# The folded matrix M in three split passes, and two feed-forward weights loaded and split later

## The reference, cut to what matters

```python
attn = jnp.einsum('bhik,bhjk->bhij', q, k)      # self-attention, 8 heads, no softmax
out = jnp.einsum('bhik,bhkj->bhij', attn, v)
...
scores = jnp.where(Mask == 0, jnp.float32(NEG_INF), scores)   # cross-attention
attn = jax.nn.softmax(scores, axis=-1)
...
r = jax.nn.sigmoid(jnp.einsum('btc,dc->btd', xr, W_r))        # feed-forward
k_act = jnp.square(jax.nn.relu(jnp.einsum('btc,dc->btd', xk, W_k)))
out = r * jnp.einsum('btc,dc->btd', k_act, W_v)
```

## Time and profile before

| what | before |
|---|---|
| median of 3 runs (lowest to highest) | 927.52 us (927.21 to 927.59) |
| time of the profiled execution | 927.58 us |
| its span | 925.8 us |
| TensorE matmuls busy | 908.7 us, 98% |
| weight loads, DVE, ACT, POOL busy | 730.2, 707.6, 545.4, 500.9 us |
| granted TensorE clock, mean | 0.998 |
| moved by DMA | 45.65 MB, 49 GB/s on average |

### The profile page before, as it was taken

One profiled execution on the slowest core, in us unless ns is written; L12 is line 12 of the kernel. 1 busy time (PEld: TensorE's weight loads), 2 busy tenths in 40 slices (PEclk: granted clock), 3 DMA queues, 4 the chain that ended last, 5 costly groups with the idle time before them and its releaser, 6 DMA issues.

```text
span 925.8 us, 18979 instructions
## 1 busy us (share of the span) xinstructions
PE 908.7 (98%) x6694; PEld 730.2 (79%) x6694; DVE 707.6 (76%) x1985; ACT 545.4 (59%) x1658; POOL 500.9 (54%) x505
## 2 busy tenths in 40 slices
PE   8999998999999999999999999999999999999997
PEld 7867566667787878888888787878787878787876
DVE  6697456457797979787887878787878787879775
ACT  6555206657665757575856666656575757575631
POOL 1034015657675666657575756666566665756420
PEclk9999999999999999999999999999999999999999
DMA  8791000103000000002101010101010010100001
GB/s 293 244 336 48 23 26 29 38 8 108 15 24 31 25 31 24 31 24 81 29 25 30 25 30 25 30 25 30 24 29 25 12 43 8 47 1 24 1 23 46
DMA packets 30890, 45.65 MB, mean 49 GB/s; under 512 B 2764, under 2 KB 15564, under 8 KB 30540
## 3 DMA queue, kind: packets, MB, share of 16 engines
q1 hardware_dynamic: 26139, 35.26, 11.9%
q10 hardware_dynamic: 4656, 9.18, 2.9%
HBM read 34.10 MB, written 9.70 MB: 47 GB/s over the span
## 4 chain that ended last, share of the span: by engine, by line
PE 73%; DVE 6%; issue 4%; POOL 3%; ACT 2%; POOLq 0%; DVEq 0%; ACTq 0%
PE dense L88 18%; PE dense L90 17%; PE dense L89 17%; PE turned L1501 5%; PE scores L1489 4%; PE rest_value L1515 3%; PE rest_value L1519 3%; PE turned L1398 1%; PE dense L1398 1%; PE rest_value L1507 1%; PE scores L1404 1%; DVE prob L1041 1%; POOL row_inv L1304 1%; ACT prob L756 1%; PE dense L1443 1%
## 5 line engine op out<-in xcount | busy, mean ns | idle before, releaser
L1304 POOL TENSOR_TENSOR row_inv<-row_sum,minus_one 128x4 f32<-128x4 f32 x128 | 145.6, 1138 | 262.5 <-ACT prob L756 260.9
L756 ACT ACTIVATE prob<-prob,row_min 128x154 f32<-128x154 f32 x512 | 209.4, 417 | 20.4 <-DVE row_min L1041 20.4
L1310 POOL TENSOR_TENSOR prob<-prob,row_inv 128x512 f32<-128x512 f32 x128 | 136.4, 1065 | 0.0
L1041 DVE CUSTOM_DVE_ANT_0 prob<-scores,mask_add 128x154 f32<-128x154 f32 x512 | 127.0, 309 | 6.3 <-PE scores L1489 6.2
L764 ACT ACTIVATE prob_t<-turned 128x512 f32<-128x512 f32 x128 | 75.8, 592 | 53.1 <-PE turned L1501 53.1
L756 ACT ACTIVATION_READ_ACCUMULATOR prob<-prob,row_min 128x1 f32 x512 | 98.8, 193 | 0.0
L1501 PE MATMUL turned<-ident,prob 128*128 128x128 f32 x512 | 77.0, 273 | 3.7 <-POOL prob L1310 1.4
L88 PE MATMUL dense<-xt_hi,cross_wq_hi 128*128 128x256 f32 x256 | 75.2, 294 | 1.3 <-DVE xt_lo L1032 1.3
L88 PE MATMUL dense<-mix_k_hi,ffn_wk_hi 128*128 128x256 f32 x256 | 74.6, 291 | 0.0
L1501 PEld LDWEIGHTS turned<-ident,prob 128*128 128x128 f32 x512 | 61.0, 141 | 15.8 <-issue 4.7
L1099 DVE TENSOR_TENSOR k_act_lo<-square,k_act_hi 128x512 fp32r<-128x512 f32 x32 | 51.4, 1606 | 28.8 <-ACT k_act_hi L789 28.8
(11 more groups left out here) (273 smaller groups left out, 2658.9 us busy)
## 6 DMA issues: line engine op xcount, KB each, us to landing
x_rows<-x_rows SPq DMA_DIRECT2D x32, 256.0 KB, 4.4
xt_raw<-x_cols SPq DMA_DIRECT2D x16, 512.0 KB, 3.7
out<-gate_then_y SPq DMA_DIRECT2D x15, 512.0 KB, 2.8
mask_in<-mask SPq DMA_DIRECT2D x16, 154.0 KB, 2.3
cross_wv<-cross_wv SPq DMA_DIRECT2D x2, 512.0 KB, 6.8
cross_wk<-cross_wk SPq DMA_DIRECT2D x1, 1024.0 KB, 9.3
self_wv<-self_wv ACTq DMA_DIRECT2D x1, 1024.0 KB, 8.0
self_wk<-self_wk ACTq DMA_DIRECT2D x1, 1024.0 KB, 11.8
```

The source lines that it names most:

```text
L756: m = act.activation(keys, keys, ACT.Exp, bias=row_min[:, buf, t, h:h + 1], scale=-1.0, accum_out=row_sum[:, buf, t, h:h + 1])
L1041: m = dve.tensor_tensor_reduce(prob[buf][:, t, h * CTX:(h + 1) * CTX], s_bank[:, h, t * CTX:(t + 1) * CTX], mask_add[n % 2][:, t, :], -SCA ...
L1304: pool.tensor_tensor(row_inv[:, buf, t, :], row_sum[:, buf, t, :], minus_one[:], ALU.pow).then_inc(*p_inv.up)
L1310: pool.tensor_tensor(keys[:, :, 0:P], keys[:, :, 0:P], inv.broadcast_to([P, HPG, P]), ALU.mult).then_inc(*p_norm.up)
```

## The change

M's quarters of both batches become three-pass products. For that self_wq is split in the prologue, and u0 and u1 are split in four parts each by ACT and DVE. The places for these parts are those of feed-forward weights, so ffn_wk and ffn_wr are no longer loaded and split in the prologue: ffn_wk is loaded first of all in the rounds and split in round -1; ffn_wr is loaded in round 1 once M is made, ahead of the write of M; ffn_wv follows, once ffn_wr has landed; both are split in round 2, at other places than ffn_wv was. The diff, cut to its core:

```diff
-    early = ("cross_wq",) + LATE_WEIGHTS[:-1]
+    early = ("cross_wq", "cross_wo")
+    splits = [weights[name] for name in early] + [(f["self_wq"], *wq_two)]
...
-            for name in early[2:]:
-                load_weight(name)
-            for i in range(len(early)):
+            for i in range(len(splits)):
                 weight_high(i)
                 high(2 * i + 24, 2 * i + 25)
+            high(30, 31)
             for q in range(KT):
                 act.wait_ge(*u_mm.at(0, q + 1))
                 act.activation(u0[:, q, :], u_bank[q][:], ACT.Copy).then_inc(*u_ok.up)
+            for q in range(KT):
+                act.wait_ge(*u_ok.at(0, q + 1))
+                act.activation(u0_two[0][:, q, :], u0[:, q, :], ACT.Copy).then_inc(*u_ok.up)
...
-            weight_low(3)
             low(30, 31)
...
+            c_times(0, 0)
+            c_times(1, 1)
+            for q in range(KT):
+                dve.wait_ge(*u_ok.at(0, KT + q + 1))
+                dve.tensor_tensor(u0_two[1][:, q, :], u0[:, q, :], f32(u0_two[0][:, q, :]), ALU.subtract).then_inc(
+                    *c_part_ok.up)
+            c_times(2, 2)
+            c_times(3, 3 + KT)
...
-                    m = pe.matmul(m_bank[i][:], f["self_wq"][:, q, i * P:(i + 1) * P], u0[:, q, :],
-                                  start=(q == 0), stop=(q == KT - 1))
+                    m = three_pass(pe, m_bank[i][:], [x[:, q, i * P:(i + 1) * P] for x in wq_two],
+                                   [x[:, q, :] for x in u0_two], first=(q == 0), last=(q == KT - 1))
...
             pe.wait_ge(*u_ok.at(0))
-            pe.wait_ge(*f_here["self_wq"].at(0))
+            pe.wait_ge(*c_part_ok.at(0, 2 + KT))
+            pe.wait_ge(*w_low.at(2))
...
+            load_weight("ffn_wk")
             load_mask(0)
...
                 if n == 1:
+
+                    sp.wait_ge(*fm_mm.at(0))
+                    load_weight("ffn_wr")
                     sp.wait_ge(*fm_eye.at(0))
                     sp.dma_start(m_park.rearrange("p (k n) -> p k n", k=KT), t1[:]).then_inc(*m_parked.up)
-                    sp.wait_ge(*fm_mm.at(0))
-                    sp.dma_start(raw["ffn_wv"][:], io["ffn_wv"].rearrange("(k p) n -> p k n", p=P)).then_inc(*w_here.up)
+                    load_weight("ffn_wv")
...
+            weight_high("ffn_wk")
             for n in range(-1, LAST):
...
                     if n == 2:
-                        weight_high()
+                        weight_high("ffn_wr")
...
                     r_gate(e, 0)
+                    if n == 2:
+                        weight_high("ffn_wv")
                     r_gate(e, 1)
...
+                if n == 0:
+                    u_high()
                 if live(n):
                     exponentials(n, 3, 0)
...
                     o_finish(f, 1)
+                if n == 2:
+                    weight_low("ffn_wr")
                 if live(f):
                     normalise(2, f, x2[f % 2])
...
                     masked_min(n, 2, 1)
-                    if n == 2:
-                        weight_low()
...
                     make_mask(a)
+                if n == 2:
+                    weight_low("ffn_wv")
                 x1t_low(a, 0)
...
                     take_t(3)
+                    weight_low("ffn_wk")
...
                     bias_u(2, 3)
+                    u_low()
...
                 if i == 0:
+                    pe.wait_ge(*fc_part.at(0))
                     pe.wait_ge(*q_out.at(1, 2))
...
-                    m = pe.matmul(m_bank[i], fold["self_wq"][:, c, i * P:(i + 1) * P], u1[:, c, :],
-                                  start=(c == 0), stop=(c == KT - 1))
+                    m = three_pass(pe, m_bank[i], [x[:, c, i * P:(i + 1) * P] for x in wq_two],
+                                   [x[:, c, :] for x in u1_two], first=(c == 0), last=(c == KT - 1))
...
-            "u": [mem.over("x1_0", "u0", square), mem.over("ffn_wv_hi", "u1", square)],
+            "u": [mem.over("x1_0", "u0", square), mem.over("ffn_wr_lo", "u1", square)],
+            "u_two": [(mem.over("ffn_wk_hi", "u0_hi", square, 0, F32R), mem.over("ffn_wk_lo", "u0_lo", square, 0, F32R)),
+                      (mem.over("ffn_wv_hi", "u1_hi", square, 0, F32R), mem.over("ffn_wr_lo", "u1_lo", square, 0, F32R))],
+            "wq_two": (mem.over("ffn_wr_hi", "self_wq_hi", square, 0, F32R), mem.over("ffn_wv_lo", "self_wq_lo", square, 0, F32R)),
```

More of the change, by code:

```diff
@@ L223, in weight_high @@
             def weight_high(i):
-                raw, hi, _ = weights[early[i]]
-                act.wait_ge(*w_here[early[i]].at(0))
+                raw, hi, _ = splits[i]
+                act.wait_ge(*(w_here[early[i]] if i < len(early) else f_here["self_wq"]).at(0))
                 act.activation(hi[:], raw[:], ACT.Copy).then_inc(*w_high.up)
@@ L307, in weight_low @@
             def weight_low(i):
-                raw, hi, lo = weights[early[i]]
+                raw, hi, lo = splits[i]
                 dve.wait_ge(*w_high.at(i))
@@ L375, in dve_program, with c_times @@
             low(28, 29)
-            weight_low(3)
             low(30, 31)
-            dve.wait_ge(*biases_in.at(0))
-            for q in range(KT):
+            def c_times(q, at):
                 dve.wait_ge(*u_ok.at(0, q + 1))
@@ L584, in layers @@
     g1, t1, kv_t1, u1 = (fold[x][1] for x in ("g", "t", "kv_t", "u"))
+    u1_two, wq_two = fold["u_two"][1], fold["wq_two"]
     s_col, s_part, c_part = (fold[x] for x in ("s_col", "s_part", "c_part"))
@@ L716, in act_program, with weight_high @@
         def act_program(act):
-            def weight_high():
-                act.wait_ge(*w_here.at(0))
-                act.activation(w["ffn_wv"][0][:], raw["ffn_wv"][:], ACT.Copy).then_inc(*w_hi_ok.up)
+            def weight_high(name):
+                act.wait_ge(*w_here.at(late.index(name)))
+                act.activation(w[name][0][:], raw[name][:], ACT.Copy).then_inc(*w_hi_ok.up)
             def take_u(*parts):
@@ L724, in take_u, with u_high @@
                     act.activation(u1[:, k, :], (d1, d0)[k % 2][:], ACT.Copy).then_inc(*fu_ok.up)
+            def u_high():
+                for k in range(KT):
+                    act.wait_ge(*fu_ok.at(0, k + 1))
+                    act.activation(u1_two[0][:, k, :], u1[:, k, :], ACT.Copy).then_inc(*fu_ok.up)
             def take_m(i):
@@ L977, in bias_u, with u_low @@
                                                  ALU.mult, ALU.add).then_inc(*fc_part.up)
+            def u_low():
+                dve.wait_ge(*fc_part.at(0, KT))
+                for k in range(KT):
+                    dve.wait_ge(*fu_ok.at(0, KT + k + 1))
+                    dve.tensor_tensor(u1_two[1][:, k, :], u1[:, k, :], f32(u1_two[0][:, k, :]), ALU.subtract).then_inc(
+                        *fc_part.up)
             def take_c():
@@ L1552, in k_product @@
             def k_product(n, h):
+                if n + h == 0:
+                    pe.wait_ge(*w_lo_ok.at(late.index("ffn_wk")))
                 pe.wait_ge(*mix_lo["k"].at(n))
@@ L1566, in r_product @@
             def r_product(n, t):
+                if n + t == 0:
+                    pe.wait_ge(*w_lo_ok.at(late.index("ffn_wr")))
                 if t == 0:
@@ L1582, in v_product @@
                 if n + t == 0:
-                    pe.wait_ge(*w_lo_ok.at(0))
+                    pe.wait_ge(*w_lo_ok.at(late.index("ffn_wv")))
                 pe.wait_ge(*ka_lo_ok.at(n))
```

30 lines of the change are left out of this document (18 added, 12 removed).

## The result

The changed kernel takes **932.08 us** (median of 7 runs, 929.62 to 935.54) against 927.59 for the kernel before on the same chip (927.21 to 928.33). The ratio is 1.0048, 95% interval 1.003 to 1.0065: half a per cent slower, where 926.2 had been forecast in a range of 924.2 to 928.9. So the time lies outside the range, on the slow side. Besides the 4.5 us there is a second thing to see: its runs lie 5.9 us apart, those of the kernel before 1.1.

What follows compares the result with a forecast made beforehand. TensorE, busy 98% of the span, was taken as the bound. The terms -0.7 + 1.4 + 0.2 - 2.1 - 0.25 = -1.45 took 927.58 to 926.2 us, range 924.2 to 928.9.

Steps and rivals of the forecast that it cites:

- The products, 2.73 us a quarter, and -0.70 each: M products on TensorE: three passes take 2.73 us a quarter instead of 3.43, saving 0.70 each.
- Quarters 0, 1 and 2 will end 2.1 us sooner, then TensorE stands still before the sums: Prologue, batch 0: the 2.1 us saved become waiting before batch 1's column sums; only quarter 3 counts, -0.70.
- The mask comes 2.8 us later: Start of the rounds: first mask queued behind ffn_wk's 1 MB, 2.8 us later; TensorE waits +1.4.
- The slack of 1.4: Start of the rounds: layer norm's first half ends 127.05, TensorE turns it at 128.51, so 1.4 us of delay is absorbed.
- +2.8 if no slack is left: Start of the rounds: upper bound of the late mask's price, +2.8 us.
- "+0.2" for round 0: Round 0: ACT's four high parts of u1 come at most 0.2 us late before the exponentials; bounds 0 and 2.2.
- -2.1 for quarters 0 to 2: Round 0, batch 1: saving of M's quarters 0 to 2 counted in full, -2.1 us.
- Quarter 3 gave nothing: Batch 1's quarter 3: next scores wait for DVE's row minima anyway, so 0, bound -0.7.
- I let the write land 0.7 us later: Round 2: write of M behind ffn_wr lands 0.7 us later; the copy behind relu still fits, 1.0 us of slack.
- the second rival: Round 2: write of M 2.7 us later delays relu, and the second split adds 1.9; total 929.9 us; chance 0.10.
- The second r product, "-0.25": Round 2: its 0.5 us weight-load wait goes as ffn_wv's split moves away; half taken, -0.25 us.
- The 250 to 850 us stretch stays full: From 250 us on TensorE stays full (0.2 us missed of 600 before); otherwise ACT, DVE or POOL lost slack.

Runs made afterwards that it cites:

- run 7: Also both_single: kernel with mask and write of M each issued ahead of its weight, but M in single fp32 products of high parts instead of three passes; 927.54 us.
- run 5: Also both: changed kernel with the mask issued ahead of ffn_wk and the write of batch 1's M ahead of ffn_wr; 927.22 us, 925.7 without low stretches.
- mask_first: Run 1: changed kernel with only the first mask issued ahead of the 1 MB of ffn_wk; 928.25 us.
- run 10: Kernel with both issue orders turned round and M's quarter 3 ahead of the column sums, ffn_wr's low part left out (VectorE split cut to 16 columns); 923.74 us against 924.47.
- after: The changed kernel itself, against the kernel before; 932.08 us against 927.59.
- after_m3: Changed kernel with only batch 0's quarter 3 of M moved ahead of the column sums, mask and write of M still behind the weights; 930.91 us.
- fill: Changed kernel with ten products into a bank nobody reads, put on TensorE ahead of the first turn of x1; 931.78 us.
- sums_first: Changed kernel with VectorE's five operations of the weights' sums ahead of the first mask, no DMA moved; 927.65 us.
- write_first: Changed kernel with only the write of batch 1's M issued ahead of ffn_wr's load; 931.75 us.
- head_alone: Kernel before plus a 1 MB load of ffn_wk into free tiles ahead of the first mask, VectorE waiting for it too; 931.65 us.
- the exchange of one line: Batch 0's quarter 3 of M moved ahead of the column sums, in the changed kernel with mask and write of M issued ahead of the weights; 924.47 us.

## Why the prediction was wrong, step by step

Three steps failed. The write of M was to land within the slack of round 2, for -0.25 us there, and round 2 took +2.8. The late mask was priced at +1.4 and made TensorE wait 2.4. And what an idle TensorE does to its own clock was priced at nothing: 3.4 us at 1.2 GHz, 1.7 to 1.8 us, in most runs. By place, in the two profiled runs, the forecast's -0.7 + 1.4 + 0.2 - 2.1 - 0.25 came out as -1.0 + 4.3 + 0.4 - 2.0 + 2.8.

The same 4.5 us by cause, all from the table's medians, some of few runs: splits and loads in the better order 0 (run 7), three passes -1.8 (run 5 against 7), the late mask +2.9 (929.8 against 926.9), the late write +1.1 (926.9 against 925.7), and the low clock +2.3 (932.1 against 929.8). The sum is 4.5. It adds up because each term is the step from one kernel to the next, and the terms are not pure: as the traces of runs 1, 5 and 7 show, 1.5 us of what the mask's edit gave back lie in round 2, the write's edit gave 0.1 there, and the three passes lost 0.9 there again.

- **The products, 2.73 us a quarter, and -0.70 each**: right.
- **"Quarters 0, 1 and 2 will end 2.1 us sooner, then TensorE stands still before the sums"**: right (the wait on the mirror additions is 1.8 us), and priced at nothing. An idle engine was counted as free; it takes TensorE's clock in most runs (8 of 11 with the stretch, 1 of 11 with it filled, 0 of 11 where the products are long enough). In the profiled run of the changed kernel it was the head's wait that did so, not this one. I looked for what is late next and not for what an idle TensorE does to itself, though the sum had in it a wait that the change makes.
- **"The mask comes 2.8 us later"**: the mechanism and the place were right, the size was not. Counted from the start of the rounds the mask came 4.0 us later (6.4 us behind it instead of 2.4). The slack of 1.4 was right: 4.0 - 1.4 = 2.6, and the profile names 2.4 as the wait. The 2.7 us came from two transfers of which the first had a start of its own and the second only its queueing time; at the head nothing was under way, and the 1 MB took 5.9 us from its issue (5.9 to 7.3 in the other runs with the weight in front). The other bound had been set at "+2.8 if no slack is left", from the same 2.8: too narrow for the same reason.
- **"+0.2" for round 0, -2.1 for quarters 0 to 2**: +0.4 and -2.0 at the fixed points (3.4 to 3.8, then to 1.8): right within 0.2. Quarter 3 gave nothing, as said.
- **"I let the write land 0.7 us later"**: this term failed, and the second rival had it. It "decides once the write lands more than 1.0 us later than today"; relu started at 234.63, 4.7 later, of which 1.8 is the offset at that point, so 2.9 later. The rival's place (relu, the copies behind it, TensorE at the transposes of 232.15, then the second split) is what the trace shows; its price was 3.5 and the profile has 2.8. Two transfers of 1 MB on one queue, 2.3 us apart, did not follow each other at 2.7 us each: the first took 6.4 us, the second 7.8, so that it landed 3.7 behind. With the write first it takes 4.9 to 6.2 us, and the loss is smaller in some traces and not in others (run 5).
- **The second r product, "-0.25"**: wrong in sign. The split of ffn_wr (2.87 us here, not 2.29) delays the y sum for which the first one waits, 0.9 us, and all of it costs +0.8 (run 10).
- **The 250 to 850 us stretch stays full**: right to the hundredth, 599.79 in both.

With the right sizes at the two transfers the forecast would have been about 930; the rest is the clock.

What stays open: why the write of M took 7.8 or 7.9 us in two traces (after, after_m3) and 6.3 in three others with the same order of issues (mask_first, fill, sums_first), why it took 6.2 in both and 4.9 in both_single, again with one order, and which of the two idle stretches took the clock in the runs that have no profile.

## What to carry to other kernels

When a change shortens work in front of a wait, the saving becomes idle time of TensorE, and idle time is not free: move useful work into the wait (here the exchange of one line: 1.2 us and a steady clock, 2.75 by the medians of all runs). A small load that is needed at once must not stand behind a large one that can wait, and a cheap guard is to put work that doesn't need it ahead of the wait. Spread between the runs is a reading of its own: the mean clock of each run showed that some 2.3 of the 4.5 us (by two runs that kept their clock) were of another kind than the stalls. And an edit that gives back the forecast number need not have done so for the forecast reason: compare the two traces place by place.

## What the hardware did unexpectedly

- TensorE's granted clock fell to 1.2 GHz for 3.4 us, or 6.8, behind idle stretches of TensorE of 1.6 us (mask_first) to 3.8 (write_first), in some executions of a kernel and not in others; each 3.4 us cost 1.7. Behind 3.4 us of idle it stayed up in the profile of head_alone. The same idle stretch of 1.8 us left the clock alone in the profiled run of the changed kernel, and took it in that of mask_first. The Trainium skill, TensorE: Matmul & The Clock Gate, What's actually happening, has the clock follow how busy TensorE has been of late; the runs agree (8 of 11 low with the idle stretch, 1 of 11 with it filled by products that compute nothing).
- 1 MB issued when no other transfer was under way took 5.9 to 7.3 us (ffn_wk in after and in write_first), and a mask of 154 KB issued 0.4 us behind it 6.0 (after) to 7.4 (write_first) until VectorE used it, instead of 2.4. Even issued 0.4 us ahead of the weight, the mask took 3.8 to 4.2 us in five traces (116.60 to 120.82 in mask_first) and 2.5 in that of both_single. The Trainium skill, DMA: Bandwidth & Descriptors, Anatomy of one DMA, gives a fit of 2.0 us and 436 GB/s for a DMA that GpSimd issues; an estimate by it is 4.4 us for 1 MB. The loads here are issued by SyncE, and their 5.9 to 7.3 us do not agree with it.
- One and the same subtraction on VectorE, 128 x 2048, took 2.28 us for ffn_wk at 137.06 and 2.87 for ffn_wr at 242.46 in one trace (after). At 137.06 GpSimd was idle. At 242.46 an operation of GpSimd had been running for 0.3 us:

```profile
242.14 1.04 POOL L1357 TENSOR_TENSOR prob<-prob,row_inv 128x512 f32<-128x512 f32 x1
```

  In both_single the split started 0.03 us ahead of the same operation, at 237.49, and took 2.29; there GpSimd's was the long one:

```profile
237.52 3.17 POOL L1357 TENSOR_TENSOR prob<-prob,row_inv 128x512 f32<-128x512 f32 x1
```

  So in these traces the one that starts second is drawn out. No run was made to test it.
